# A convolution kernel on one core: the last unit's stores are issued image by image from three queues

## The reference

```python
kern = construct_kernel(weight, P)        # (32, 32, 7, 7), bilinear scatter of 9 points
out = conv_general_dilated(_gn(x), kern, stride 1, padding 3) + bias
return x + out                            # (32, 32, 56, 56) float32
```

## Time and profile before

| | us |
|---|---|
| median of 3 runs | 320.62 |
| lowest and highest of them | 320.38, 321.65 |
| the profiled execution, its time | 321.43 |
| its span, first to last instruction | 319.6 |
| TensorE busy in it | 288.1 (90%) |
| mean granted clock of TensorE | 0.956 |

### The profile page before, as it was taken

How to read it: one execution, slowest core, us unless ns; L and a number is a source line. 1 busy time by engine, 2 the same in 40 slices (tenths; PEclk the granted TensorE clock), 3 DMA queues, 4 the chain that set the end, 5 groups by cost and what they waited for, 6 DMA issues and landing times.

```text
span 319.6 us, 9702 instructions
## 1 busy us (share of the span) xinstructions
PE 288.1 (90%) x3436; PEld 201.4 (63%) x3436; DVE 266.9 (84%) x358; ACT 225.1 (70%) x327; POOL 177.8 (56%) x339
## 2 busy tenths in 40 slices
PE   4930699799999999999999999999999899999990
PEld 2710466567666677777766777777777577776760
DVE  5359598999898999999998989999999799996221
ACT  2259897878878796969696978888787769570300
POOL 6342646656565849393948566565657392934000
PEclk9585599999999999999999999999999999999997
DMA  8952445979999898989999979999998949498605
GB/s 143 156 108 58 119 134 116 245 181 213 224 211 241 185 251 168 264 177 240 196 235 199 258 162 229 224 220 229 216 237 183 251 98 229 104 236 221 131 2 102
DMA packets 128255, 59.09 MB, mean 185 GB/s; under 512 B 122068, under 2 KB 122068, under 8 KB 128228
## 3 DMA queue, kind: packets, MB, share of 16 engines
q1 hardware_dynamic: 115204, 24.90, 42.0%
q0 software_dynamic: 9312, 33.04, 39.1%
q10 hardware_dynamic: 3712, 0.80, 1.4%
HBM read 12.88 MB, written 12.85 MB: 81 GB/s over the span
## 4 chain that ended last, share of the span: by engine, by line
PE 70%; DMA 5%; POOL 5%; issue 1%; DVE 1%; DVEq 0%; ACT 0%; POOLq 0%
PE ps_eo L796 22%; PE ps_x L796 17%; PE ps_s L796 17%; PE ps_y L796 13%; DMA xb<-xs 5%; POOL xn L704 2%; POOL xb L673 1%; PE ps_stat L741 1%; DVE xs L457 1%; POOL rtmp L679 1%; DVE result L461 1%; POOL rtmp L681 0%; DVEq L54 0%; ACT rinv L320 0%; DVE var L431 0%
## 5 line engine op out<-in xcount | busy, mean ns | idle before, releaser
L673 POOL DMA_DIRECT2D xb<-xs x192 | 94.1, 496 | 55.6 <-DVE xs L457 52.6
L796 PE MATMUL ps_eo<-xs,w 128*64 128x392 f16 (+1 forms) x576 | 98.7, 324 | 0.0
L796 PE MATMUL ps_eo<-xb,w 128*64 128x392 f16 (+1 forms) x576 | 98.7, 324 | 0.0
L796 PEld LDWEIGHTS ps_eo<-xb,w 128*64 128x64 f16 x576 | 61.6, 109 | 18.3
L796 PE MATMUL ps_s<-xb,w 128*64 128x392 f16 (+1 forms) x384 | 69.9, 332 | 3.1 <-DMA xb<-xs 3.1
L796 PE MATMUL ps_s<-xs,w 128*64 128x392 f16 (+1 forms) x384 | 70.4, 332 | 0.1
L796 PE MATMUL ps_x<-xb,w 128*64 128x392 f16 x384 | 67.7, 328 | 0.0
L796 PE MATMUL ps_x<-xs,w 128*64 128x392 f16 x384 | 67.7, 328 | 0.0
L344 ACT ACTIVATE xs<-e 128x900 f16<-128x900 f32 x48 | 59.4, 1238 | 11.3 <-DVE e L434 8.8
L796 PEld LDWEIGHTS ps_eo<-xs,w 128*64 128x64 f16 x576 | 61.7, 109 | 7.2
L457 DVE TENSOR_TENSOR xs<-e,xs 128x900 f16<-128x900 f32 x48 | 64.8, 1349 | 0.1
(11 more groups left out here) (90 smaller groups left out, 450.5 us busy)
## 6 DMA issues: line engine op xcount, KB each, us to landing
xb<-xs POOLq DMA_DIRECT2D x96, 168.8 KB, 4.2
xb<-xs POOLq DMA_DIRECT2D x96, 166.9 KB, 4.6
xraw<-x SPq DMA_DIRECT2D x124, 98.0 KB, 3.0
out<-result SPq DMA_DIRECT2D x124, 98.0 KB, 4.5
xraw<-x ACTq DMA_DIRECT2D x4, 98.0 KB, 4.0
out<-result ACTq DMA_DIRECT2D x4, 98.0 KB, 3.7
wnat<-L_conv_weight POOLq DMA_DIRECT2D x1, 36.0 KB, 3.5
pts<-L_conv_P POOLq DMA_DIRECT2D x2, 1.1 KB, 2.9
```

The source lines that it names most:

```text
L673: pool.dma_start(dst[32 * g:32 * g + 32, 0:run - line * past], src[32 * f:32 * f + 32, line * past:run]).then_inc(shifted[par][b], DMA)
L796: last = pe.matmul(into[p:p + HALF, :, 0:PER * wide], w[:, n // 2, s, q, t, :], moving.rearrange("p n q m -> p n (q m)"), start=fresh and ...
```

## The change

Four calls of `last_store` take the place of two and a fifth is added; each has an image and a list of groups, and waits for that image alone (`combined` at 111 for image 0, at 112 for image 1).

- SP: image 0, groups 0 and 1; then image 1, group 0.
- ScalarE: image 0, groups 2 and 3; then image 1, group 1.
- GpSimd: image 1, groups 2 and 3, at the end of its program, after the last `shift`.

GpSimd's two stores raise a semaphore of their own, `stored_last`, for which SP waits at the end together with the other two. The bytes, the runs of 224 bytes and the number of stores stay the same.

```diff
+        stored_last = sem("stored_last")
...
-        def put(queue, u, par, m, g):
+        def put(queue, u, par, m, g, done=None):
             queue.dma_start(dram_rows(out, u, m, g),
                             result[32 * g:32 * g + 32, par, PLANE * m:PLANE * (m + 1)].rearrange(
-                                "c (n w) -> c n w", w=SIDE)).then_inc(stored[par], DMA)
-
-        def last_store(queue, first):
-
-            queue.wait_ge(combined, OUTS * UNITS)
-            for m in range(PER):
-                for g in (first, first + 2):
-                    put(queue, UNITS - 1, (UNITS - 1) % 2, m, g)
+                                "c (n w) -> c n w", w=SIDE)).then_inc(stored[par] if done is None else done, DMA)
+
+        def last_store(queue, m, groups, done=None):
+
+            queue.wait_ge(combined, OUTS * UNITS - 1 + m)
+            for g in groups:
+                put(queue, UNITS - 1, (UNITS - 1) % 2, m, g, done)
...
-            last_store(sp, 0)
-            for par in range(2):
-                sp.wait_ge(stored[par], LOAD * (UNITS // 2))
+            last_store(sp, 0, (0, 1))
+            last_store(sp, 1, (0,))
+            sp.wait_ge(stored[0], LOAD * (UNITS // 2))
+            sp.wait_ge(stored[1], LOAD * (UNITS // 2) - 2 * DMA)
+            sp.wait_ge(stored_last, 2 * DMA)
...
-            last_store(act, 1)
+            last_store(act, 0, (2, 3))
+            last_store(act, 1, (1,))
...
                 shift(u, u % 2, 2)
+            last_store(pool, 1, (2, 3), stored_last)
```

## The result

The change makes the kernel slower: 322.90 us median of 12 runs (321.52 to 325.83) against 321.18 us (319.49 to 324.03) of 12 runs of the kernel before; the ratio is 1.0067 (95% interval 1.004 to 1.0094). Forecast were 320.1 us, in a range of 319.3 to 321.3. The forecast was counted from 320.62 us, the median of the first three runs of the kernel before, so 0.56 of the 2.8 us between forecast and measurement lie in that base.

What follows compares the result with a forecast made beforehand. TensorE, busy 288.1 of 319.6 us, was taken as the bound and untouched; only the tail would move. -0.54 (early start) + 0 (GpSimd's stores) + 0.03 (added wait) = -0.51 us from 320.62 gave 320.1 us, range 319.3 to 321.3.

Steps and rivals of the forecast that it cites:

- The reading of the tail: After the last matmuls: VectorE's halves, 1.2 us issue to data, 4.4 us data, 0.8 us landing, 0.5 us block end.
- early start: SP's and ScalarE's first stores, of image 0, issue at 312.15 instead of 312.69 us: -0.54 us.
- rival C: Tail: no gain, the early start is eaten by a drain longer than 4.4 us; 320.6 us, chance 0.15.
- The extrapolated price of GpSimd's issue: GpSimd's stores of 448 runs, extrapolated from DMAs with fewer runs: 1.07 us a store, 0.62 to 1.61.
- landing formula: GpSimd's second store lands at 312.69 plus two issues plus 1.9 us: 316.7 us, before the other stores.
- Rival A: Tail: GpSimd's stores cost the DMA engines less and fill the ramp; -1.0 us, 319.6 us, chance 0.17.
- The added wait: SP's wait for one more semaphore at the end, already passed when reached: +0.03 us.
- GpSimd is free: End of GpSimd's program: last shift DMAs issued by 294.6 us, so its wait holds up nothing and it issues at 312.69.
- Part 2: Two stores move from the two hardware queues to GpSimd at the end: counted as 0.
- part 3: SP waits for one more semaphore at the end, raised before the others: +0.03 us.
- G over 3 us or an unseen cost: GpSimd's issue of one store over 3 us, or a cost not seen: slower than 322.2 us, chance 0.06.
- Rival B: GpSimd's second store lands last, later than before from an issue of 2.25 us; 321.7 us at 2.8 us, chance 0.13.

Runs made afterwards that it cites:

- e1: Changed kernel with GpSimd's two stores given back to SP and ScalarE, order by image kept: 320.93 us, ratio 0.9982, then 320.37 us, ratio 0.9986.
- e8: Changed kernel with a DRAIN of GpSimd's own ahead of its two stores, in its idle time: 320.73 us, ratio 1.0023.
- e12: Changed kernel, but GpSimd stores two groups of image 0, with its own DRAIN ahead: 320.54 us, ratio 0.9965, then 321.27 us, ratio 1.000.

## Why the prediction was wrong

**The reading of the tail** held: VectorE's pair, 1.2 us to the first data, 4.4 us of data, 0.8 us to the landing. So did the **early start** as a mechanism: 0.54 us earlier issue and earlier data in every kernel with the order by image. Its worth was over-sized: 0.54 us forecast, 0.2 to 0.3 measured in e1 and 0.4 in e8. The term took the data's 4.4 us as given; it is 4.7 in e1 and 4.6 in the changed kernel. That is the sign that **rival C** named, a drain longer than 4.4 us, but it eats a part of the gain and not all of it.

**The extrapolated price of GpSimd's issue** was 1.07 us a store (0.62 to 1.61); it is 0.64 and 0.67, near the lower end, and landing was no trouble:

```profile
L196 POOL DMA_DIRECT2D out<-result x2: 638/655/672, 312.3 to 312.9; - x2
...
DMA to landing us min/median/max: 3.5/3.8/4.0
```

They land by 312.9 + 4.0 = 316.9, where the landing formula with the measured issue gives 312.3 + 1.3 + 1.9 = 315.5. The formula took copies that ran alone; these share the engines. It does not matter, since the other stores end at 318.1. **Rival A** found no cheaper drain: the changed kernel's stretch (data from 312.7 to 317.3) is 4.6 us long at a share of 0.91, 4.2 us of full engines as before. That agrees with the rule of the Trainium skill that the prediction cites ("DMA: Bandwidth & Descriptors", "Issuing engines are not separate DMA queues"): all queues run on the same 16 engines. **The added wait** of SP's cost nothing that can be seen.

**The step that failed** is the sentence "GpSimd is free ... so its wait for `combined` holds up nothing behind it". I asked what stands behind the wait in the source, and found nothing. In the trace something stood there: the closing DRAIN of 7,562 ns, in the rows of the block's end, which the prediction left unread because SP's wait there was 0.2 us. Part 2 and part 3 put GpSimd's end at nothing; it cost 2.0 us. The sum with that row and the measured issues: image 1 is complete at 310.88 + 1.16 = 312.04; GpSimd's stores start 0.29 us later, take 1.28 and the DRAIN 7.1 more, and the end follows after 0.2: 320.9. Counted from image 1, that is 8.9 us against 319.6 - 312.67 = 6.9 before: 1.9 to 2.0 us more. The prediction's own numbers with the row (a DRAIN that ends 7.0 us after the last instruction, 294.0 + 7.6 against 294.6) give 312.69 + 2 x 1.07 + 7.0 + 0.2 = 322.0, that is 2.4 us more than the span of 319.6: the right sign, and too much mostly by the over-sized issue. A slowdown over 0.5% had a chance of 0.06 there, for "G over 3 us or an unseen cost"; it was the unseen cost. **Rival B** had the right place, GpSimd as the last to end, and a wrong mechanism: it needed an issue of 2.25 us, and the issue was a third of that.

Had GpSimd been given work that ends 7.3 us before the end of the span, nothing would have been seen of this. From its last instruction to the end of the tail before there are 8.09 - 0.2 - 7.1 = 0.8 us from the pair's start (an estimate from these rows): GpSimd's program may end that late and no later.

## What to carry to other kernels

Before work is given to an engine that is idle at the end, look up in the trace what that engine still does after its last instruction; idle time can be the cover of its own ending. Read the block's end per engine, also where nobody waits for it yet. When a third queue is tried for transfers that already keep the DMA engines full, only an earlier start can pay (0.4 us here, in e8), and two queues give most of that as well (0.2 to 0.3 us, in e1).

## What the runs showed of the hardware

- GpSimd's closing DRAIN took 0.17 us plus 82 ns for every DMA that GpSimd had issued since its last DRAIN, though all had landed: measured with 0, 2, 6, 16 and 96 DMAs of 32 runs each. With 195 it was 7.04 us, less than with 96, and in the middle of the kernel 99 DMAs cost 9.4 us from the last issue; both for reasons that stay open. A DRAIN in idle time clears the account (7.6 us there, and then 0.17).
- With two stores in flight after such a clearing, the DRAIN ended about when the last one had landed (e8: 316.4 and 316.3; e12: 316.6 and 316.5, then 318.8 and 318.7). What stores of 448 runs cost it once they have landed was not measured.
- A GpSimd DMA of 448 runs of 224 bytes was issued in 0.64 to 0.67 us, against 0.49 for 32 long runs: 416 more runs cost 0.15 to 0.18 us, 0.4 ns a run.
- With image 0's stores 0.54 us earlier the data of all eight took 4.7 us on two queues instead of 4.4; on three, in the changed kernel, 4.6.
